# Attention on one core: the product of probabilities and ones set directly behind the product with the values

## The chip, the cores and the metric

One core of a Trainium2 chip runs the kernel. The metric is device time in microseconds (us), the median of several runs. Five engines work side by side and meet through semaphores: TensorE (PE, with its weight loads shown as PEld), VectorE (DVE), ScalarE (ACT), GpSimd (POOL) and the DMA queues, most of them fed by SyncE (SP).

## The reference

The layer is a gated cross-attention followed by a gated mixture of experts, over 8 sequences of 512 tokens of width 512. The change touches the attention alone:

```python
Q = proj(query, Wq, bq); K = proj(key, Wk, bk); V = proj(value, Wv, bv)   # 16 heads of 32
scores = jnp.einsum('bhqd,bhkd->bhqk', Q, K) / SCALE
attn = jax.nn.softmax(scores, axis=-1)
out = jnp.einsum('bhqk,bhkd->bhqd', attn, V)
...
x = x + jnp.tanh(g_xattn[0]) * _L0_xattn_ref(_layernorm(x), ctx_1024, ctx_1024, ...)
x = x + jnp.tanh(g_ffn[0]) * _L0_ffn_ref(_layernorm(x), ...)   # router, top 2 of 8 experts
```

## The kernel before

The program first runs the attention for 8 batches one after another (batch 0, a loop over batches 1 to 6, batch 7), then the router and the 8 experts. The order of every engine's work is written out by hand.

A batch of the attention begins with the projections of queries and keys. They are split into two float16 parts and stacked by DMA in `stk`, so that one matmul of 96 rows gives the scores of a head in full precision. Then come 23 steps, s = 0 to 22 (`SLOTS`), and after them the output product (L1346). A step holds work of three ages:

- `scores(s, qt)` (L1227), for s below 16: head s, 128 queries x 512 keys. There are four of them, qt = 0 to 3, each of one matmul, and they write only two PSUM banks: qt 0 and 2 bank 0, qt 1 and 3 bank 1. DVE takes the row maxima out of each (`mx`, L838) and frees the bank; before TensorE writes the next scores there, `claim` makes it wait for that.
- `less_maxima(u, hf)` (L1237), u = s - 6: the transposed scores with the maxima already taken off, for a group of four heads and 128 keys, in two halves of two matmuls. ACT turns each half into probabilities `pt` (the exponential, L718). The halves write banks 2 and 3, and 4 and 5.
- `with_values` (L1246) and `with_ones` (L1253), v = s - 7: the probabilities of the step before times the values, into bank 6, and times ones, which gives the sums of the softmax, into bank 7. Each has one matmul for each of the four heads of the group; each of these writes 32 partitions, and the four stand in four column tiles of the array. They are float32, and the trace counts each as two instructions. The last one of `with_ones` raises `pv_done`.

Ahead of `with_values` TensorE waits until ACT has read both halves of the step before (`copied`), and in steps 11, 15 and 19, where a new group of heads begins, until ACT has copied banks 6 and 7 to `osum` (L726). That copy stands on ACT behind both exponentials of its step, 10, 14 and 18 (L718 first, then L726).

In steps 4, 8, 12 and 16 a transpose of the maxima (L1318) goes through bank 0 as well; DVE reads it in two instructions (L859, L861) that stand between its maxima of qt 0, 1 and of qt 3, 2. In these steps TensorE computes qt 3 ahead of qt 2. In steps 16 to 22 of all batches but the last, TensorE also transposes the inputs of the next batch (L1154). DVE further has the reciprocals of the sums (L850), the product with them (L878) and the statistics of the next batch.

Of the kernel before, what the change touches and what calls it, by code (L numbers as in the profile page):

```python
# [43 lines left out]
LAG_B, LAG_C = 6, 7  # L44
# [39 lines left out]
def layer_kernel(nc, x, ctx_in, g_x, g_f, Wq, bq, Wk, bk, Wv, bv, Wo, bo, Wr, br, W1, b1, W2, b2, out):  # L84
# [8 lines left out]
    with stack:  # L93
# [195 lines left out]
        def copied(eng, where, key, b=0):  # L289

            bank, n = where(key, b)
            eng.wait_ge(bank_read[bank], n + 1)
# [850 lines left out]
        def _(pe):  # L1143
# [68 lines left out]
            def batch(b, last_batch, first=False):  # L1212
                rows, parts, logits = router(use, b, KT * b)
                for i, (which, m) in enumerate(QK_ORDER):
                    n = "qk".index(which)
                    if m == 0:
                        for kt in range(KT):
                            copied(pe, act_use, ("actT", n, kt), b)
                    dst, full = claim(pe, use, ("qk", i), b)
                    product(dst, [(wT[:, n, wp, kt, m * P:(m + 1) * P], actT[:, n, xp, kt, :])  # L1220
                                  for kt in range(KT) for wp, xp in PARTS]).then_inc(full, 1)

                def scores(s, qt):

                    if s < UNITS:
                        dst, full = claim(pe, use, ("S", s, qt), b)
                        t_.matmul(dst, stk[0:96, 0, s, qt * P:(qt + 1) * P], stk[0:96, 1, s, :],  # L1227
                                  start=True, stop=True).then_inc(full, 1)

                def less_maxima(u, hf):  # L1230

                    if 0 <= u < UNITS:
                        g, kt = u // 4, u % 4
                        _, full = claim(pe, use, ("ST", u, hf), b)
                        for j in range(2):
                            h = 4 * g + 2 * hf + j
                            last = t_.matmul(psum[:, 2 + 2 * hf + j, :], stk[0:98, 1, h, kt * P:(kt + 1) * P],  # L1237
                                             stk[0:98, 0, h, :], start=True, stop=True)
                        last.then_inc(full, 1)

                def with_values(u):
                    if 0 <= u < UNITS:
                        g, kt = u // 4, u % 4
                        for j in range(4):
                            h = 4 * g + j
                            t_.matmul(psum[32 * j:32 * j + 32, 6, :], v32[:, kt, HD * h:HD * h + HD],  # L1246
                                      pt[:, (2 * u + j // 2) % 4, j % 2, :], start=(kt == 0), stop=(kt == KT - 1))

                def with_ones(u):
                    if 0 <= u < UNITS:  # L1250
                        kt = u % 4
                        for j in range(4):
                            last = t_.matmul(psum[32 * j:32 * j + 32, 7, :], ones32[:, :],  # L1253
                                             pt[:, (2 * u + j // 2) % 4, j % 2, :], start=(kt == 0), stop=(kt == KT - 1))
                        last.then_inc(pv_done, 1)

                def values(tt, half):

                    if half == 0:
                        claim(pe, use, ("v", tt), b)  # L1260
                    bank, _ = use(("v", tt), b)
                    for kt in (2 * half, 2 * half + 1):
                        for xp, wp in PARTS:
                            last = t_.matmul(psum[:, bank, :], actT[:, 1, xp, kt, tt * P:(tt + 1) * P], wT[:, 2, wp, kt, :],
                                             start=(kt == 0 and (xp, wp) == (0, 0)),
                                             stop=(kt == KT - 1 and (xp, wp) == (1, 0)))
                    if half == 1:
                        last.then_inc(bank_full[bank], 1)

                if first:  # L1270
                    pe.wait_ge(k_ones, 1)
                for s in range(SLOTS):

                    if s == 0:
                        pe.wait_ge(stk_q0, 12 * 16 * b + 12 * 16)
                    if s < 4:
                        pe.wait_ge(stk_k0[s], 3 * 16 * b + 3 * 16)
                    if s == 4:
                        dmas = (12 + 3 * len(SP_HEADS)) * 16
                        pe.wait_ge(stk_rest, dmas * b + dmas)  # L1280
                        dmas = 3 * len(POOL_HEADS) * 16
                        pe.wait_ge(stk_rest_pool, dmas * b + dmas)
                    scores(s, 0)
                    scores(s, 1)
                    if s == X2T_SLOT:
                        rows()
                    for tt in range(KT):
                        if s in V_HALF[tt]:
                            values(tt, V_HALF[tt].index(s))
                    if s == LG_SLOT:  # L1290
                        parts()
                    u = s - LAG_B
                    if 0 <= u < UNITS and u % 4 == 0:
                        pe.wait_ge(mrow_in[u // 4], 32 * b + 32)
                    less_maxima(u, 0)
                    if not last_batch and s > UNITS:
                        for i in act_tiles(s):
                            inputs_transposed(b + 1, i // KT, i % KT)
                    if 0 <= s - LAG_C < UNITS:
                        v_ = s - LAG_C  # L1300
                        if v_ < KT:
                            copied(pe, use, ("v", v_), b)
                        if v_ % 4 == 0:

                            if v_ == 0:
                                pe.wait_ge(norm_done, NG * b)
                            else:
                                pe.wait_ge(osum_ready, (NG - 1) * b + v_ // 4)
                        for hf in range(2):
                            copied(pe, use, ("ST", v_, hf), b)  # L1310
                    with_values(s - LAG_C)
                    if s % 4 == 0 and 4 <= s <= UNITS:
                        g = s // 4 - 1

                        for qt in (2, 3):
                            copied(pe, use, ("S", 4 * g + 3, qt), b)
                        dst, full = claim(pe, use, ("mT", g), b)
                        t_.transpose(dst[0:16, 0:P], mx[:, 16 * g:16 * g + 16], ident[:, :]).then_inc(full, 1)  # L1318
                    if not last_batch and s == UNITS:
                        for i in act_tiles(s):  # L1320
                            inputs_transposed(b + 1, i // KT, i % KT)
                    if s % 4 == 0:

                        less_maxima(u, 1)
                        scores(s, 3)
                        scores(s, 2)
                    else:
                        scores(s, 2)
                        less_maxima(u, 1)
                        scores(s, 3)  # L1330
                    for tt in range(KT):
                        if V_HALF[tt] == (s, s):
                            values(tt, 1)
                    if s == LG_SLOT:
                        logits()
                    with_ones(s - LAG_C)
                for gs in (range(KT - 1), range(KT - 1, KT)):
                    for tt in range(KT):
                        if gs[0] == 0:
                            claim(pe, use, ("o", tt), b)  # L1340
                        bank, _ = use(("o", tt), b)
                        for kt in gs:
                            if tt == 0:
                                pe.wait_ge(a_ready, NG * b + kt + 1)
                            for ap, wp in PARTS:
                                last = t_.matmul(psum[:, bank, :], aT[:, ap, kt, tt * P:(tt + 1) * P], wT[:, 3, wp, kt, :],  # L1346
                                                 start=(kt == 0 and (ap, wp) == (0, 0)),
                                                 stop=(kt == KT - 1 and (ap, wp) == (1, 0)))
                        if gs[0] == KT - 1:
                            last.then_inc(bank_full[bank], 1)  # L1350
# [146 lines left out]
```

## Time and profile before

| | us |
|---|---|
| median of 3 runs | 2117.45 |
| range of the 3 runs | 2116.48 to 2123.11 |
| span of the profiled execution, first to last instruction | 2114.6 |
| median less that span | 2.85 |
| PE busy | 1856.6 (88%) |
| DVE busy | 1260.1 (60%) |
| ACT busy | 690.7 (33%) |
| POOL busy | 743.9 (35%) |

The page gives no time of the profiled execution beyond its span. The attention fills about the first 990 us; the router and the experts follow. A busy share is a mean over the whole span, so what matters for one step of the attention has to be read from the order in time inside that step.

### The profile page before, as it was taken

The page shows a single profiled execution, that of the slowest core. Times are in us where ns is not written, and L with a number is a line of the kernel's source. Part 1 is how long each engine was busy: PE and PEld are TensorE (multiplying, and loading weights), DVE is VectorE, ACT ScalarE, POOL GpSimd, SP SyncE. Part 2 cuts the span into 40 slices and gives each one's busy share as a digit, 9 for nine tenths or more (in the row PEclk, how much of TensorE's full clock was granted, in tenths as well). Part 3 has the DMA queues.
Part 4 walks back from the last instruction along what each step waited for, and adds up shares of the span by engine and source line. Part 5 has one row for each costly group of instructions (what it writes and reads, how often), then busy time and mean ns, then how long its engine had stood idle before and what let it go on. Part 6 is the DMA issues. An engine that isn't in the chain of part 4 may idle for free. (4 is left out here: it accounts for less than half of the span.)

```text
span 2114.6 us, 31511 instructions
## 1 busy us (share of the span) xinstructions
PE 1856.6 (88%) x10838; PEld 956.6 (45%) x10838; DVE 1260.1 (60%) x2128; ACT 690.7 (33%) x884; POOL 743.9 (35%) x650
## 2 busy tenths in 40 slices
PE   7999999999999999996029898998988988898996
PEld 4333242423333242422016565565655656565674
DVE  5776768686776868675856445462544635445330
ACT  4443535344443536343204123031321303123030
POOL 2424233433424233412324334242442524334241
PEclk9999999999999999998559999999999999999998
DMA  5214131211314131222201324223342322324211
GB/s 184 61 43 118 41 102 38 78 62 52 107 40 119 40 84 36 49 72 78 88 24 61 95 79 129 64 78 81 92 110 63 118 57 92 96 78 128 64 41 25
DMA packets 116959, 162.23 MB, mean 77 GB/s; under 512 B 45236, under 2 KB 63040, under 8 KB 112808
## 3 DMA queue, kind: packets, MB, share of 16 engines
q1 hardware_dynamic: 72488, 134.00, 20.0%
q0 software_dynamic: 44416, 27.50, 6.8%
q8 instruction: 34, 0.56, 0.1%
q14 instruction: 21, 0.17, 0.0%
HBM read 108.92 MB, written 26.85 MB: 64 GB/s over the span
## 5 line engine op out<-in xcount | busy, mean ns | idle before, releaser
L1429 PE MATMUL psum<-xgT,w 128*128 128x308 f16 (+1 forms) x3072 | 437.8, 300 | 3.8 <-ACT h L768 3.2
L1451 PE MATMUL psum<-w,hT 128*123 128x512 f16 x1920 | 433.0, 387 | 3.3 <-PE psum L1391 3.3
L838 DVE TENSOR_REDUCE mx<-psum 128x1 f32<-128x512 f32 x512 | 328.8, 684 | 151.5 <-PE psum L1227 150.3
L1429 PEld LDWEIGHTS psum<-xgT,w 128*128 128x128 f16 x3072 | 296.5, 99 | 116.4 <-ACT h L768 3.5
L1451 PEld LDWEIGHTS psum<-w,hT 128*123 128x123 f16 x1920 | 263.2, 139 | 159.2 <-issue 15.2
L628 POOL TENSOR_TENSOR hT<-h,hT 128x615 f16<-128x615 f32 x128 | 221.2, 1728 | 278.0 <-DVE hT L1106 278.0
L718 ACT ACTIVATE pt<-psum 128x1024 f32<-128x1024 f32 x256 | 259.3, 1022 | 171.1 <-PE psum L1237 171.1
L768 ACT ACTIVATE h<-psum,b1c 128x308 f32<-128x308 f32 (+1 forms) x256 | 117.7, 514 | 539.5 <-PE psum L1429 485.6
L638 POOL DMA_INDIRECT out_dram<-y,idx_now x40 | 102.3, 2558 | 331.5 <-DVE y L1134 243.2
L1227 PE MATMUL psum<-stk 96*128 96x512 f16 x512 | 173.0, 384 | 33.3 <-DVE mx L838 14.3
L1106 DVE CAST hT<-h 128x615 f16<-128x615 f32 x128 | 63.3, 495 | 198.5 <-ACT h L768 198.5
L752 ACT ACTIVATE w<-stage 128x2048 f16<-128x2048 f32 x64 | 122.2, 1909 | 177.0 <-DMA stage<-in_L_ffn_W_dram 177.0
L1149 PE MATMUL psum<-actT,wT 128*128 128x512 f16 x768 | 167.1, 379 | 2.0 <-DVE wT L825 2.0
L1081 DVE SCALAR_TENSOR_TENSOR w<-stage,w 128x512 f16<-128x512 f32 x240 | 165.8, 722 | 0.3
L1061 DVE TENSOR_SCALAR hot<-iota_p,p_e 128x123 bf16<-128x123 bf16 x256 | 162.2, 722 | 0.0
L1237 PE MATMUL psum<-stk 98*128 98x512 f16 x512 | 153.6, 381 | 0.0
L1131 DVE SCALAR_TENSOR_TENSOR y<-psum,b2b 123x512 f32<-123x512 f32 x40 | 27.7, 692 | 198.0 <-PE psum L1451 198.0
L1246 PE MATMUL psum<-pt,v 128*32 128x512 f32 x1024 | 136.4, 605 | 5.3 <-ACT osum L726 5.0
L1253 PE MATMUL psum<-pt,ones 128*32 128x512 f32 x1024 | 136.2, 604 | 0.0
L541 POOL TENSOR_SCALAR a<-t,bias 128x512 f32<-128x512 f32 x32 | 22.3, 697 | 317.2 <-DVE t L878 317.2
L1227 PEld LDWEIGHTS psum<-stk 96*128 96x128 f16 x512 | 43.9, 96 | 198.2 <-DVE mx L838 132.4
L1086 DVE COPY xgT<-psum 128x615 f16<-128x615 f16 x64 | 28.9, 479 | 149.5 <-PE psum L1406 149.1
(177 smaller groups left out, 1860.6 us busy)
## 6 DMA issues: line engine op xcount, KB each, us to landing
stage<-in_L_ffn_W_dram SPq DMA_DIRECT2D x64, 1024.0 KB, 5.3
stk<-qks SPq DMA_DIRECT2D x120, 96.0 KB, 2.8
xin<-in_x_dram SPq DMA_DIRECT2D x8, 1024.0 KB, 5.1
cin<-in_ctx_dram SPq DMA_DIRECT2D x8, 1024.0 KB, 5.3
xres<-in_x_dram SPq DMA_DIRECT2D x8, 1024.0 KB, 5.7
out_dram<-xres SPq DMA_DIRECT2D x32, 256.0 KB, 2.1
x_split<-x2hl SPq DMA_DIRECT2D x32, 256.0 KB, 2.2
stk<-qks POOLq DMA_DIRECT2D x72, 96.0 KB, 3.8
```

The costliest lines, as they stand in the source:

```text
L628: g.tensor_tensor(hT[:, 1, m, :], h32[:, m % 4, :], hT[:, 0, m, :], ALU.subtract).then_inc(h_ready, 1)
L718: s.activation(pt[:, (2 * u + hf) % 4, :, :], psum[:, bank:bank + 2, :], ACT.Exp, scale=1.0 / (math.sqrt(HD) * SQ * SQ)).then_inc(read, 1)
L838: v.reduce_max(mx[:, KT * t + qt:KT * t + qt + 1], ps, AX.X).then_inc(read, 1)
L1061: v.tensor_scalar(hot[:, t % HOT, :], iota_p[:, :], p_e[:, t:t + 1], None, ALU.is_equal).then_inc(hot_ready, 1)
L1081: v.scalar_tensor_tensor(part[1], stage[:, i % 2, cols], SW, part[0], ALU.mult, ALU.subtract).then_inc(chunk_split, 1)
L1149: last = t_.matmul(dst, lhsT, rhs, start=(i == 0), stop=(i == len(pairs) - 1))
L1227: t_.matmul(dst, stk[0:96, 0, s, qt * P:(qt + 1) * P], stk[0:96, 1, s, :], start=True, stop=True).then_inc(full, 1)
L1237: last = t_.matmul(psum[:, 2 + 2 * hf + j, :], stk[0:98, 1, h, kt * P:(kt + 1) * P], stk[0:98, 0, h, :], start=True, stop=True)
L1246: t_.matmul(psum[32 * j:32 * j + 32, 6, :], v32[:, kt, HD * h:HD * h + HD], pt[:, (2 * u + j // 2) % 4, j % 2, :], start=(kt == 0), stop=( ...
L1253: last = t_.matmul(psum[32 * j:32 * j + 32, 7, :], ones32[:, :], pt[:, (2 * u + j // 2) % 4, j % 2, :], start=(kt == 0), stop=(kt == KT - 1))
L1429: mm = t_.matmul(psum[:, (2 * m + ch) % 4, 0:c1 - c0], w1[:, wp, kt, m * P:(m + 1) * P], xgT[:, xp, kt, c0:c1], start=(kt == 0 and (wp, xp ...
L1451: mm = t_.matmul(psum[0:CP, Y_BANK[c], :], hT[:, hp, k, c * CP:(c + 1) * CP], w2[:, wp, k, :], start=(k == 0 and (hp, wp) == (0, 0)), stop ...
```

## The change

`with_ones` of a step is called directly behind `with_values` of the same step and no longer at the end of the step. Nothing is added or removed, and the waits and semaphores of each instruction stay the same.

```diff
@@ -1309,6 +1309,7 @@
                         for hf in range(2):
                             copied(pe, use, ("ST", v_, hf), b)
                     with_values(s - LAG_C)
+                    with_ones(s - LAG_C)
                     if s % 4 == 0 and 4 <= s <= UNITS:
                         g = s // 4 - 1
 
@@ -1333,7 +1334,6 @@
                             values(tt, 1)
                     if s == LG_SLOT:
                         logits()
-                    with_ones(s - LAG_C)
                 for gs in (range(KT - 1), range(KT - 1, KT)):
                     for tt in range(KT):
                         if gs[0] == 0:
```

Only TensorE's queue has another order. On it, a step with scores and the beginning of the next (steps 11 and 12 of a batch) read before, with L1227 the scores, L1237 those with the maxima off, L1246 the product with the values, L1253 that with ones, L1318 the transpose of the maxima:

```order
L1237 MATMUL psum<-stk 128x512 x2
L1246 MATMUL psum<-pt,v 32x512 x4
L1227 MATMUL psum<-stk 128x512
L1237 MATMUL psum<-stk 128x512 x2
L1227 MATMUL psum<-stk 128x512
L1253 MATMUL psum<-pt,ones 32x512 x4
L1227 MATMUL psum<-stk 128x512 x2
L1237 MATMUL psum<-stk 128x512 x2
L1246 MATMUL psum<-pt,v 32x512 x4
L1318 MATMUL psum<-ident,mx 16x128
```

The same place on TensorE after the change (the transpose is now at L1319):

```order
L1237 MATMUL psum<-stk 128x512 x2
L1246 MATMUL psum<-pt,v 32x512 x4
L1253 MATMUL psum<-pt,ones 32x512 x4
L1227 MATMUL psum<-stk 128x512
L1237 MATMUL psum<-stk 128x512 x2
L1227 MATMUL psum<-stk 128x512 x3
L1237 MATMUL psum<-stk 128x512 x2
L1246 MATMUL psum<-pt,v 32x512 x4
L1253 MATMUL psum<-pt,ones 32x512 x4
L1319 MATMUL psum<-ident,mx 16x128
```

The last two scores of a step and the first two of the next, which had the product with ones between them, now stand side by side: the row "x3" holds the fourth score of one step and the first two of the next.

On TensorE in the steps without scores (17 and 18 of a batch that is not the last; L1154 is the transpose of the next batch's inputs), before:

```order
L1237 MATMUL psum<-stk 128x512 x2
L1154 MATMUL psum<-ident,xn 128x128 x4
L1246 MATMUL psum<-pt,v 32x512 x4
L1237 MATMUL psum<-stk 128x512 x2
L1253 MATMUL psum<-pt,ones 32x512 x4
L1237 MATMUL psum<-stk 128x512 x2
L1154 MATMUL psum<-ident,xn 128x128 x4
L1246 MATMUL psum<-pt,v 32x512 x4
```

And after:

```order
L1154 MATMUL psum<-ident,xn 128x128 x4
L1246 MATMUL psum<-pt,v 32x512 x4
L1253 MATMUL psum<-pt,ones 32x512 x4
L1237 MATMUL psum<-stk 128x512 x4
L1154 MATMUL psum<-ident,xn 128x128 x4
L1246 MATMUL psum<-pt,v 32x512 x4
```

Between the second half of the scores with the maxima off and the product with values that needs its exponential, the product with ones no longer stands; what is left there is the next step's first half (in the same row, "x4") and the transpose.

## Rows read from the trace of the kernel before

**Rows 1.** The page: TensorE's busy share and granted clock in 40 slices.

```profile
PE   7999999999999999996029898998988988898996
PEclk9999999999999999998559999999999999999998
```

**Rows 2.** Stretches of the span: engines' busy time, granted clock, DMA share.

```profile
core 0: us, PE busy (x) PEld busy (x) DVE busy (x) ACT busy (x) POOL busy (x), PEclk, DMA share, GB/s
438.87:471.88 33.01, 32.39 (x198) 7.72 (x194) 27.64 (x48) 18.76 (x19) 15.76 (x16) 1.00 0.02 8
471.88:496.14 24.26, 24.09 (x174) 7.57 (x170) 18.71 (x28) 14.26 (x15) 3.72 (x4) 1.00 0.13 44
950.68:972.05 21.37, 20.49 (x141) 3.83 (x138) 8.47 (x12) 14.17 (x15) 3.71 (x4) 1.00 0.01 1
```

**Rows 3.** Timeline, TensorE, one regular step: start, length, what, idle before it.

```profile
443.14 0.60 PE L1227 MATMUL psum<-stk 96*128 96x512 f16 x2
443.59 0.60 PE L1237 MATMUL psum<-stk 98*128 98x512 f16 x2
444.11 1.07 PE L1246 MATMUL psum<-pt,v 128*32 128x512 f32 x8
445.11 0.39 PE L1227 MATMUL psum<-stk 96*128 96x512 f16 x1
445.34 0.60 PE L1237 MATMUL psum<-stk 98*128 98x512 f16 x2
445.77 0.38 PE L1227 MATMUL psum<-stk 96*128 96x512 f16 x1
446.08 1.06 PE L1253 MATMUL psum<-pt,ones 128*32 128x512 f32 x8
447.08 0.39 PE L1227 MATMUL psum<-stk 96*128 96x512 f16 x1
```

**Rows 4.** Timeline, TensorE, end of a batch: the two products side by side.

```profile
494.28 1.06 PE L1246 MATMUL psum<-pt,v 128*32 128x512 f32 x8
495.16 1.04 PE L1253 MATMUL psum<-pt,ones 128*32 128x512 f32 x8
496.14 1.04 PE L1346 MATMUL psum<-wT,aT 128*128 128x512 f16 x4
```

**Rows 5.** Timeline, TensorE, end of step 5 and start of step 6.

```profile
430.91 0.60 PE L1227 MATMUL psum<-stk 96*128 96x512 f16 x2
432.07 0.39 PE L1227 MATMUL psum<-stk 96*128 96x512 f16 x1 [0.57 <-DVE mx L838]
432.67 0.39 PE L1227 MATMUL psum<-stk 96*128 96x512 f16 x1 [0.21 <-DVE mx L838]
```

**Rows 6.** Timeline: first users of a score and of a second half, and reciprocals.

```profile
445.54 0.69 DVE L838 TENSOR_REDUCE mx<-psum 128x1 f32<-128x512 f32 x1 [0.30 <-PE psum L1227]
446.03 1.02 ACT L718 ACTIVATE pt<-psum 128x1024 f32<-128x1024 f32 x1 [0.79 <-PE psum L1237]
454.99 0.94 DVE L850 RECIPROCAL osum<-osum 128x128 f32<-128x128 f32 x1
```

**Rows 7.** Timeline, step 8: the transpose of the maxima and what follows it.

```profile
440.83 0.28 PE L1318 MATMUL psum<-ident,mx 128*16 128x128 f32 x1
441.79 0.10 PEld L1227 LDWEIGHTS psum<-stk 96*128 96x128 f16 x1 [0.53 <-DVE mrow L861]
441.80 0.69 DVE L838 TENSOR_REDUCE mx<-psum 128x1 f32<-128x512 f32 x1
```

**Rows 8.** Timeline, step 11: ACT's copy of the sums and TensorE's wait.

```profile
451.23 1.02 ACT L726 ACTIVATE osum<-psum 128x1024 f32<-128x1024 f32 x1 [0.24 <-PE psum L1253]
452.15 1.02 ACT L718 ACTIVATE pt<-psum 128x1024 f32<-128x1024 f32 x1
452.31 0.64 PE L1246 MATMUL psum<-pt,v 128*32 128x512 f32 x4 [0.25 <-ACT osum L726]
```

**Rows 9.** Timeline, TensorE, last batch: a second half, and the values that need it.

```profile
968.33 0.60 PE L1237 MATMUL psum<-stk 98*128 98x512 f16 x2
968.86 1.06 PE L1253 MATMUL psum<-pt,ones 128*32 128x512 f32 x8
970.20 1.06 PE L1246 MATMUL psum<-pt,v 128*32 128x512 f32 x8 [0.27 <-ACT pt L718]
```

**Rows 10.** The page: the count of the moved instructions.

```profile
L1253 PE MATMUL psum<-pt,ones 128*32 128x512 f32 x1024 | 136.2, 604 | 0.0
```

## The prediction

> **What bounds the kernel now.** I read the slices first: during the attention TensorE is busy 90% or more in nearly every slice, at a granted clock of 1.00, so at the 2.4 GHz level [rows 1, 2]. The chain that ended last covers only 4% of the span and says nothing of the attention. So I went to the stretches and the timeline. Steps 8 to 15 of a batch take 33.01 us, with TensorE busy 32.39; steps 16 to 22 take 24.26 us with 24.09 busy [rows 2]. TensorE is the bound there, and nobody delivers late. The reader should then see why nobody is late. In a regular step (3.94 us from 443.14 to 447.08) two tiled products of 1.0 us each stand between pairs of scores [rows 3]. The scores have two banks only. While the product with values runs, DVE empties the banks of qt 0 and 1; while the product with ones runs, it empties those of qt 2 and 3. The same product also covers ACT's exponential of the second half. The change takes this second cover away and puts it on top of the first.
>
> **What the change gives.** The 1,024 counted instructions [rows 10] are 8 per step, 128 steps, 16 per batch. Alone, a tiled product takes 1.00 us until the next float16 matmul starts (444.11 to 445.11) and 0.09 more ahead of it (the pair from 443.59 takes 0.52 where the one from 445.34 takes 0.43) [rows 3]. Side by side the first takes 0.88 and the second 0.98, together 1.86 [rows 4]; I use 1.87. So TensorE's own work falls by 2.00 + 0.09 - 1.87, about 0.22 us a step. Step 22 has the two side by side already, so 15 steps of a batch move: 15 x 8 x 0.22 = 26 us to be won if nothing waits.
>
> The Trainium skill (TensorEngine Tiling (Array Packing), Key Properties) says that changing the tiling mode drains the engine. The 0.12 and 0.09 us above bear it out, and by that rule alone the change should be faster; that is my first rival.
>
> **What it costs in steps with scores (7 to 15).** Between steps 5 and 6 no product stands yet: the last two scores of step 5 start at 430.91, the first of step 6 follows 1.16 us later (432.07) and its second 0.60 after that (432.67), each waiting for DVE [rows 5]. That is the neighbourhood that the change makes in the later steps, with the same banks in the same turn (the fourth score there comes 0.66 behind the third, still in time for DVE's second reading). So I take 1.16 from the third score of a step to the first of the next and 1.76 to its second. Before, the distances were 1.97 (445.11 to 447.08) and about 2.2, and no wait showed. The relative times of a regular step are now: first score 0, second 0.60 (held by DVE; 0.22 if free), first half 0.82, values 1.34 (0.52 later), both products 1.87, third score 3.21, next first score 3.21 + 1.16 = 4.37. Against 3.94 that is +0.43.
>
> - A step with the transpose (8, 12): it starts at 3.21, and DVE can begin on the scores behind it 0.97 later, at 4.18 (441.80 - 440.83, [rows 7]). The second half fills 3.32 to 3.75 and the fourth score starts at 3.76. In this turn the next first score needs the bank that is read second: 3.76 + 1.76 = 5.52. Its own second score is then free as well, so the step after (9, 13) has it at 0.22: values 0.96, third score 2.83, next step at 3.99.
> - Steps 11 and 15 wait for the copy of sums. It stands on ACT behind the exponential of the second half. That exponential starts 0.69 behind its matmuls (446.03 - 445.34) [rows 3, 6]; the next on ACT follows 0.92 later (452.15 - 451.23), and values may start 1.08 behind the copy's start (452.31 - 451.23) [rows 8]. So values start no sooner than 0.69 + 0.92 + 1.08 = 2.69 after the second half, 2.92 after the third score (0.23 between them). Unheld they would start 1.16 + 1.34 = 2.50 after it. +0.43, so the step takes 4.80. The earlier end of the product with ones doesn't help, since the copy is queued behind the later exponential.
> - Steps 8 to 15: 5.52 + 3.99 + 4.37 + 4.80 + 5.52 + 3.99 + 4.37 + 4.52 (step 15 ends without a next score: 3.64 + 0.88) = 37.08, against 33.01: +4.07. Step 7: third score 0.87 later, next step 1.16 behind it instead of 1.97: +0.06. Together +4.13 per batch.
>
> **What it costs in steps 16 to 22.** There, values wait for the exponential of the last second half: 1.87 us from the start of its matmuls to values (968.33 to 970.20), the wait showing as ACT pt [rows 9]. TensorE has 0.44 (rest of the half) + 0.44 + 0.53 (next half, transposes of the inputs) = 1.41 to fill it, so it idles 0.46. From one second half to the next: 1.87 + 1.87 = 3.74 (about 3.5 before); in step 19, with the copy of sums, 2.69 + 1.87 = 4.56. From the start of step 16: its values at +1.22 (1.87 behind a half that started 0.65 earlier), its second half at 1.22 + 1.87 + 0.11 + 0.44 = 3.64, then 3.74 + 3.74 + 4.56 + 3.74 + 3.74 to that of step 21 at 23.16, values of step 22 at 25.03, output product at 26.89. Against 24.26: +2.63. In the last batch there are no transposes: 1.22 + 1.87 + 0.11 = 3.20, + 19.52 = 22.72, + 1.87 + 1.86 = 26.45, against 21.37: +5.08 [rows 2].
>
> **The sum.** 7 x (4.13 + 2.63) + (4.13 + 5.08) = 47.3 + 9.2 = 56.5 us. The span would go from 2114.6 to 2171.1; the median of the runs lies 2.85 above the profiled span, so 2174. Of this the won 0.22 us a step is already taken off. DVE's and ACT's queues and all DMAs keep their order, and steps 0 to 6, the projections and everything behind the attention are untouched. The output product needs the same last sums in the same order. The transpose of the maxima and the mrow DMA behind it move later in their step, but the steps that use them, two on, move too.
>
> **Bounds.** The weakest terms are those where DVE or ACT has other work. Behind the maxima of step 11 come two reciprocals; one takes 0.94 [rows 6]. The maxima end 1.76 behind the third score, so the reciprocals end near 3.6, the next two maxima near 4.9, and the transposed maxima of step 12 are ready at 1.16 + 3.21 + 0.28 = 4.65: up to 0.25 late, or nothing. I take nothing; 0.25 to 0.5 in four steps of each batch is up to 16 us. To the other side, the distances of ACT could be shorter by 0.1 in the ten held steps, and the waits for the copy may be met halfway: up to 8 x 2 = 16 us.
>
> **Rivals.**
> 1. *Faster, through the spared switches.* For it: the 0.22 us a step, read from rows. It decides if DVE frees a bank within the 0.88 us that TensorE then needs from a third score to the next first one (0.23 + 0.43 + 0.22), instead of 1.16, and the second within 1.10 instead of 1.76. Against it stand both distances behind step 5 [rows 5]. It would give 2117.45 - 26 = 2091.
> 2. *Only the banks count, the ACT side is absorbed.* The +4.13 of steps 7 to 15 stays less the 0.43 in two steps, and steps 16 to 22 go on as before because the transposes and the next half cover the exponential: 8 x 3.3 = 26, so 2144. Against it: 1.41 of cover to 1.87 needed.
> 3. *DVE falls behind for good.* The reciprocals and the statistics now collide with earlier scores, and the upper bound holds or is passed: 2190 and above. For it: DVE is busy 27.64 of 33.01 us [rows 2]; against it: the new step is longer, 37.08, for the same work.
> 4. *The clock.* More gaps in TensorE's work could cost the granted clock. The rows show 1.00 throughout, TensorE's short waits of step 5 among them; it falls only where TensorE's busy digit falls to 6 and 0, behind the attention [rows 1]. If it fell, it would be tens of us more.
> 5. *No change*: waits and spared switches cancel. They would have to be equal, and the rows give 0.43 against 0.22 at least, after the gain is counted.
>
> **Chances.** Forecast (2160 to 2188): 0.74. Rival 1: 0.05. Rival 2: 0.09. Rivals 3 and 4: 0.10. Rival 5: 0.02. The range 2152 to 2191 leaves the lower part of rival 2, rival 1 and most of 4 outside. Within 0.3% (6.4 us) is about what a measurement can tell from no change. Faster 0.05, same 0.02, slower 0.93.
>
> **What would show it.** The third score to the next first one at 1.16 us, with a wait for DVE's maxima of 0.3 us, and 0.4 us ahead of the second; a regular step of 4.37, one with a transpose of 5.52; values held by ACT pt for 0.4 us in steps 17, 18, 20 and 21 and by the copy of sums for some 1.3 us in step 19; values to ones 0.88. In the grouped lines, idle time of TensorE ahead of L1227 should rise from DVE by roughly 8 x 5 us, and PE's busy time should fall by some 25. If regular steps take 3.7 us the prediction is wrong and rival 1 right; if steps 16 to 22 still take 24 us, rival 2.

## The result, and the profile after

The changed kernel takes 2181.57 us (median of 4 runs, 2177.17 to 2185.44), the kernel before 2116.97 beside it: a ratio of 1.0297, 95% interval 1.0273 to 1.0321. That is 64.6 us more, where 57 had been forecast (2174, range 2152 to 2191). In a later series the same pair gave 2180.41 to 2120.4, a ratio of 1.0276 (1.0259 to 1.0294), 60.0 us more. The profiled execution has a span of 2183.5 us, 68.9 above the one of before. It is the slowest of its four (2185.44, 3.9 above the median), so about 4 of the 68.9 us are the choice of the execution.

The page's slices after, TensorE's busy share and granted clock, to be held against [rows 1]: the busy share is 8 in many slices of the attention that had 9, and the attention is longer.

```profile
PE   7898898989889898988306999898988988898997
PEclk9999999999999999999656999999999999999999
```

The same three stretches as in [rows 2], in the profile after (steps 8 to 15, steps 16 to 22, steps 16 to 22 of the last batch):

```profile
462.92:500.22 37.30, 32.51 (x194) 9.05 (x195) 27.43 (x47) 18.38 (x19) 15.70 (x16) 1.00 0.02 5
500.22:527.02 26.80, 23.00 (x171) 9.13 (x169) 20.03 (x30) 14.90 (x16) 3.72 (x4) 1.00 0.13 39
1010.25:1036.60 26.35, 19.48 (x139) 5.25 (x137) 9.56 (x14) 14.79 (x16) 3.71 (x4) 1.00 0.00 1
```

The first is 37.30 us long against 33.01 and the second 26.80 against 24.26. TensorE was idle in them for 0.62 and 0.17 us before and is idle for 4.8 and 3.8 now, while its busy time in the second falls by 1.1 and in the first rises by 0.1. In the last batch the stretch is 26.35 us long against 21.37.

The grouped lines of TensorE before, of the scores and the product with values:

```profile
L1227 PE MATMUL psum<-stk 96*128 96x512 f16 x512 | 173.0, 384 | 33.3 <-DVE mx L838 14.3 <-DMA stk<-qks 12.0 <-DVE mrow L861 4.3
L1246 PE MATMUL psum<-pt,v 128*32 128x512 f32 x1024 | 136.4, 605 | 5.3 <-ACT osum L726 5.0 <-ACT pt L718 0.3
```

And after; the line numbers of these three didn't change:

```profile
L1227 PE MATMUL psum<-stk 96*128 96x512 f16 x512 | 181.9, 386 | 68.0 <-DVE mx L838 42.1 <-DMA stk<-qks 13.0 <-DVE mrow L861 4.3
L1246 PE MATMUL psum<-pt,v 128*32 128x512 f32 x1024 | 136.4, 603 | 37.6 <-ACT pt L718 23.3 <-ACT osum L726 14.4
L1253 PE MATMUL psum<-pt,ones 128*32 128x512 f32 x1024 | 134.5, 592 | 0.0
```

The moved instructions [rows 10] still wait for nobody. The waits are in front of their neighbours: the scores wait 42.1 us for DVE's maxima instead of 14.3, and the product with values waits 37.6 us for ACT instead of 5.3, 23.3 of it for the exponentials and 14.4 for the copy of the sums. The wait for DMA, 13.0, is nearly what it was (12.0).

Steps 9 to 11 on TensorE after, which answer to [rows 3] (start, length, what, and the idle time just before):

```profile
469.50 1.06 PE L1246 MATMUL psum<-pt,v 128*32 128x512 f32 x8
470.38 1.04 PE L1253 MATMUL psum<-pt,ones 128*32 128x512 f32 x8
471.36 0.39 PE L1227 MATMUL psum<-stk 96*128 96x512 f16 x1
471.58 0.60 PE L1237 MATMUL psum<-stk 98*128 98x512 f16 x2
472.02 0.91 PE L1227 MATMUL psum<-stk 96*128 96x512 f16 x2
473.19 0.39 PE L1227 MATMUL psum<-stk 96*128 96x512 f16 x1 [0.26 <-DVE mx L838]
473.41 0.60 PE L1237 MATMUL psum<-stk 98*128 98x512 f16 x2
473.94 1.07 PE L1246 MATMUL psum<-pt,v 128*32 128x512 f32 x8
...
478.71 1.07 PE L1246 MATMUL psum<-pt,v 128*32 128x512 f32 x8 [0.26 <-ACT osum L726]
```

Values to ones is 0.88 us as in [rows 4]. The third score starts at 471.36. The row "472.02 ... x2" holds two scores that do not follow one another at once: its length of 0.91 instead of 0.60 is the wait for the first bank (0.14), folded in, and the second of the two starts at 472.53. The next step's second score starts at 473.19, 1.83 behind the third score. A step from values to values is 4.44 us (469.50 to 473.94) and, with the wait for the copy, 4.77 (473.94 to 478.71). It was 3.94 and 4.26.

Step 8 after, which answers to [rows 7]:

```profile
466.22 0.28 PE L1319 MATMUL psum<-ident,mx 128*16 128x128 f32 x1
...
466.77 0.80 PE L1227 MATMUL psum<-stk 96*128 96x512 f16 x2
468.53 0.60 PE L1227 MATMUL psum<-stk 96*128 96x512 f16 x2 [0.96 <-DVE mx L838]
```

From the score of qt 3 (466.77), which this step computes ahead of qt 2, to the next first one (468.53) there are 1.76 us, with 0.96 of plain waiting. Steps 17 to 19 after, the answer to [rows 9] for a batch with transposes:

```profile
505.70 1.07 PE L1246 MATMUL psum<-pt,v 128*32 128x512 f32 x8 [0.40 <-ACT pt L718]
506.56 1.07 PE L1253 MATMUL psum<-pt,ones 128*32 128x512 f32 x8
507.56 1.04 PE L1237 MATMUL psum<-stk 98*128 98x512 f16 x4
508.43 0.60 PE L1154 MATMUL psum<-ident,xn 128*128 128x128 f32 x4
509.43 1.06 PE L1246 MATMUL psum<-pt,v 128*32 128x512 f32 x8 [0.39 <-ACT pt L718]
...
513.98 1.06 PE L1246 MATMUL psum<-pt,v 128*32 128x512 f32 x8 [1.22 <-ACT osum L726]
```

Each step takes 3.73 us instead of 3.50, and values wait 0.4 us for the exponential; in step 19 they wait 1.22 us for the copy.

Because the four transposes of the maxima (steps 4, 8, 12, 16) and the output product show in every batch, their starts cut each batch into stretches that can be compared between runs. A length says what the change costs only over a whole batch: where the product with ones of step 8 or 16 is moved, it stands ahead of that step's transpose, so 0.9 us is counted one stretch earlier, and where the values are late, they stand behind it and count one stretch later. Lengths in us, of batches 1 to 6, where they agree within 0.03, and of batch 7; the last column is how many batches from 1 on show a granted clock of 0.5 for 3.4 us behind the DMA wait of step 4:

| kernel | 4 to 8 | 8 to 12 | 12 to 16 | 16 to output | sum | batch 7, sum | at 0.5 |
|---|---|---|---|---|---|---|---|
| before | 13.92 | 16.51 | 16.07 | 22.72 | 69.22 | 66.17 | 0 |
| changed | 15.28 | 18.78 | 18.29 | 23.73 | 76.08 | 75.61 | 3 |
| only steps 7 to 15 | 15.28 | 18.78 | 17.43 | 22.72 | 74.21 | 71.22 | 0 |
| only steps 16 to 22 | 13.92 | 16.52 | 16.92 | 23.73 | 71.09 | 72.13 | 0 |
| changed, half first | 14.46 | 17.51 | 17.48 | 23.73 | 73.18 | 72.76 | 1 |
| changed, short maxima | 13.64 | 17.41 | 17.31 | 23.73 | 72.09 | 71.62 | 1 |
| before, short maxima | 12.68 | 16.38 | 15.87 | 22.72 | 67.65 | 64.65 | 5 |
| changed, copy first | 15.28 | 18.45 | 17.95 | 23.24 | 74.92 | 74.38 | 1 |
| both at the end | 13.78 | 16.50 | 15.73 | 22.20 | 68.21 | 63.70 | 0 |
| values late, with step 7 | 14.57 | 16.15 | 14.71 | 22.21 | 67.64 | 63.12 | 1 |
| values late, without step 7 | 13.92 | 16.15 | 14.71 | 22.20 | 66.98 | 63.35 | 1 |

For the changed kernel this gives 6 x 6.86 + 9.44 (batch 7) + 6.94 (batch 0, 75.98 to 69.04) = 57.5 us. Of the other 11.4 us between the two spans, 1.35 lie ahead of batch 0's step 4, 5.7 between an output product and step 4 of the next batch (seven times) and 4.4 behind the attention. The 1.35 go with the clock as well: the changed kernel's profile has 3.4 us at 0.5 there, behind a wait of 1.99 us for DVE. Nine of the thirteen profiles have them, with step 4 of batch 0 at 68.27 to 70.33 us; the other four, the one of before among them, have the same wait without them, and step 4 at 67.02 to 67.98.

### The profile page after: what moved, and what is told of

Same layout as the page of the kernel before. It is cut to its first block and busy times, and to the rows that moved or that the text cites. A ratio compares the mean times of both kernels' runs of the same rounds, so it can differ in the third digit from the quotient of the medians.

```text
span 2183.5 us, 31511 instructions
## 1 busy us (share of the span) xinstructions
PE 1858.8 (85%) x10838; PEld 982.2 (45%) x10838; DVE 1259.4 (58%) x2128; ACT 685.5 (31%) x884; POOL 743.8 (34%) x650
## 5 line engine op out<-in xcount | busy, mean ns | idle before, releaser
L1227 PE MATMUL psum<-stk 96*128 96x512 f16 x512 | 181.9, 386 | 68.0 <-DVE mx L838 42.1
L1246 PE MATMUL psum<-pt,v 128*32 128x512 f32 x1024 | 136.4, 603 | 37.6 <-ACT pt L718 23.3
L1227 PEld LDWEIGHTS psum<-stk 96*128 96x128 f16 x512 | 48.0, 96 | 219.5 <-DVE mx L838 123.8
L1237 PE MATMUL psum<-stk 98*128 98x512 f16 x512 | 146.6, 380 | 0.0
L1253 PE MATMUL psum<-pt,ones 128*32 128x512 f32 x1024 | 134.5, 592 | 0.0
L1149 PEld LDWEIGHTS psum<-actT,wT 128*128 128x128 f16 x768 | 75.3, 98 | 94.0 <-issue 4.4
```

The lines of the kernel that those rows point to most:

```text
L1149: last = t_.matmul(dst, lhsT, rhs, start=(i == 0), stop=(i == len(pairs) - 1))
```

## The experiments

**The change in half of the steps.** With the scores (steps 7 to 15) and without them (16 to 22), as two kernels; the diff is the first, and the second has the two conditions exchanged.

```diff
                     with_values(s - LAG_C)
-                    with_ones(s - LAG_C)
+                    if s < UNITS:
+                        with_ones(s - LAG_C)
...
+                    if s >= UNITS:
+                        with_ones(s - LAG_C)
```

> The product with ones stands directly behind the product with values only in steps below 16, where scores are left; in steps 16 to 22 it stands as in the kernel before. Bank theory (the scores have two banks, and DVE's maxima no longer finish behind a product): regular steps of 4.44 us instead of 3.94, those with the transpose of the maxima near 5.7, +4.3 us a batch, so +34 us in all, near 2151, with TensorE's waits in steps 16 to 22 gone. Rival (the two tiled products side by side are themselves slow): the loss goes by the number of moved steps, 9 of 15, so +39 us. Rival (only the exponential counts): near 0.

Measured: 2161.29 us to 2119.2, ratio 1.020 (1.0178 to 1.0221), +42.1 (40.0 in the stretches). The mechanism's +34 was too low, and the rival that the pair is slow (+39) isn't refuted by this run alone; the last batch of the next run and the kernel with both products at the end decide against it.

> The reverse: moved only in steps 16 and up. Exponential theory: values wait 0.4 us in steps 17, 18, 20, 21 and 22 and 1.2 us in step 19; +2.5 us in each of seven batches and +5 in the last, which has no transposes to fill the gap: +23 us, near 2140. Rival (the pair itself is slow, per step): 6 of 15 steps, +26 us, but the last batch like the others. Rival (only the banks count): -10 us, the spared changes of tiling.

Measured: 2139.78 us to 2119.2, ratio 1.0091 (1.007 to 1.0113), +20.6. In its last batch, where no transposes fill the gap, the trace shows

```profile
984.29 1.04 PE L1237 MATMUL psum<-stk 98*128 98x512 f16 x4
986.17 1.06 PE L1246 MATMUL psum<-pt,v 128*32 128x512 f32 x8 [0.83 <-ACT pt L718]
```

a wait of 0.83 us where the other batches have 0.4. The two parts add up (4.99 + 1.87 = 6.86 a batch; 42.1 + 20.6 = 62.7 us in all), so they don't act on each other. The tail's loss follows the gap, 1.87 us in six batches and 5.96 in the last, and not the number of moved steps: the same six steps move in each. Of the 5.96, some 1.65 is half clock in that batch (24.94 us from step 16 to the output, 23.29 in the changed kernel at full clock), so the gap costs 4.3. The split is 5.0 to 1.9 a batch where 4.3 to 2.5 was expected. I had booked the wait at step 16 under the tail, but it comes whenever step 15 has its product with ones moved: with steps 7 to 15 alone, the values of step 16 wait 0.61 us for the exponential.

**Other work into the gap.** The changed kernel, with the first half ahead of the first two scores.

```diff
+                    u = s - LAG_B
+                    if 0 <= u < UNITS and u % 4 == 0:
+                        pe.wait_ge(mrow_in[u // 4], 32 * b + 32)
+                    less_maxima(u, 0)
                     scores(s, 0)
                     scores(s, 1)
...
-                    less_maxima(u, 0)
```

> The changed kernel, with the first half of the scores with the maxima off put ahead of the first two scores of each step, so that 0.44 us of other work stands where TensorE waits for DVE. Bank theory: the step of 4.44 us falls to 4.00, in steps that do not wait for the copy of sums; about 6 steps of a batch x 0.44 x 8 = 21 us back, near 2160, and steps 16 to 22 as in the changed kernel. Rival (the pair of products is slow in itself, or the waits only look like DVE's): no change from 2182.

Measured: 2150.61 us, ratio to before 1.0142 (1.0118 to 1.0166); the changed kernel had 1.0297 and 1.0276. A regular step on TensorE:

```profile
458.95 0.39 PE L1227 MATMUL psum<-stk 96*128 96x512 f16 x1
...
459.83 0.59 PE L1237 MATMUL psum<-stk 98*128 98x512 f16 x2
460.27 0.90 PE L1227 MATMUL psum<-stk 96*128 96x512 f16 x2
461.10 1.07 PE L1246 MATMUL psum<-pt,v 128*32 128x512 f32 x8
461.98 1.04 PE L1253 MATMUL psum<-pt,ones 128*32 128x512 f32 x8
462.95 0.39 PE L1227 MATMUL psum<-stk 96*128 96x512 f16 x1
```

It takes 4.00 us (458.95 to 462.95), as the bank account says: the same DVE wait, partly filled. The stretches give 2.9 us a batch, 23 in all, against 21 expected; the medians differ by some 30, of which the rest lies outside the stretches, some 4 of it the half clock behind step 4's wait (one batch against three). Steps 16 to 22 are unchanged (23.73).

**A faster DVE.** Both orders with maxima over 128 of the 512 keys; the maxima of the other keys are left out.

```diff
-                            v.reduce_max(mx[:, KT * t + qt:KT * t + qt + 1], ps, AX.X).then_inc(read, 1)
+                            v.reduce_max(mx[:, KT * t + qt:KT * t + qt + 1], ps[:, 0:128], AX.X).then_inc(read, 1)
```

> The changed kernel, but DVE takes the maxima over the first 128 of 512 keys only (the maxima of the other keys are left out), so that it frees a bank some 0.4 us sooner. Bank theory: the third score to the next first one takes 0.88 instead of 1.16 us (TensorE's own work), the next second one waits 0.25 instead of 0.43, a regular step 3.95 instead of 4.44, the one with the transpose 4.9 instead of 5.74; the steps with scores cost 1 us a batch more than before instead of 4.3, steps 16 to 22 still +2.5. Against the kernel before with the same short maxima: +28 us instead of +65. Rival (the product pair, or TensorE's queue, is what is slow): still +60 or more.

> The kernel before with the same short maxima over 128 keys (the maxima of the other keys are left out), as the base for the run with the changed order. Both theories: regular steps stay at 3.94 us, since the product with ones covers DVE anyway; only the steps with the transpose of the maxima and steps 1 to 7 gain, together up to 2 us a batch: 2100 to 2115.

Measured: 2149.57 us (1.0132, 1.0114 to 1.0151) and 2116.83 (0.9976, 0.9964 to 0.9987) to 2121.44, the second above the 2100 to 2115 expected. The order alone now costs 32.7 us, about half, where 28 had been expected. From the first of the two:

```profile
454.24 0.39 PE L1227 MATMUL psum<-stk 96*128 96x512 f16 x1
...
455.67 0.39 PE L1227 MATMUL psum<-stk 96*128 96x512 f16 x1 [0.17 <-DVE mx L838]
...
456.42 1.07 PE L1246 MATMUL psum<-pt,v 128*32 128x512 f32 x8
...
461.19 1.07 PE L1246 MATMUL psum<-pt,v 128*32 128x512 f32 x8 [0.66 <-ACT osum L726]
```

From the third score to the next second one there are 1.43 us instead of 1.83, and the regular step is 4.04 us (452.38 to 456.42, the values of steps 9 and 10) instead of 4.44; 3.95 had been expected. Where values wait for the copy nothing is gained: the step stays at 4.77 and the wait grows from 0.26 to 0.66, since ACT's copy ends 2.9 us behind the third score whatever DVE does. Against the kernel before with short maxima, the stretches 4 to 16 cost 3.4 us more. Of that 0.9 is the place of step 16's product with ones, ahead of the transpose, which leaves 2.5 for the steps with scores, not the 1 us that I had expected: the two waits for the copy, in steps 11 and 15, cost 0.5 and 0.6 more than there (steps of 4.77 to 4.26 and 4.18), and values of step 16 wait 0.61 for the exponential. The other 0.8 is not accounted for. By the stretches the order still costs 7 x 4.4 + 7.0 = 38 us, where it cost 57.5; the medians differ by less, and in the profile of the kernel before with short maxima the DMA wait of step 4 is 2.3 to 2.9 us long and the clock falls behind it in five batches, about 1.7 us each, against one in the other.

**The copy of the sums earlier on ACT.** The changed kernel with `osum` between the two exponentials of its step.

```diff
+                        if t in GROUP_END[:-1] and hf == 0:
...
+                            s.activation(osum[:, :, :], psum[:, 6:8, :], ACT.Copy).then_inc(osum_ready, 1)
-                    if t in GROUP_END[:-1]:
...
-                        s.activation(osum[:, :, :], psum[:, 6:8, :], ACT.Copy).then_inc(osum_ready, 1)
```

> The changed kernel, with ACT's copy of the sums ahead of the second exponential of its step instead of behind it. Queue theory (in steps 11, 15 and 19 values wait for the copy only because it stands behind a late exponential): no wait in steps 11 and 15 (0.26 us each), in step 19 values start 2.2 instead of 2.7 us behind the second half: 1 us a batch, 8 in all, near 2173. Rival (the copy is late because ACT is short of time): no change.

Measured: 2167.87 us, ratio to before 1.0224 (1.0203 to 1.0245). In step 10 ACT now does

```profile
471.05 1.02 ACT L725 ACTIVATE osum<-psum 128x1024 f32<-128x1024 f32 x1 [0.94 <-PE psum L1252]
471.97 1.02 ACT L718 ACTIVATE pt<-psum 128x1024 f32<-128x1024 f32 x1
```

and values of step 11 start without a wait. The stretches shrink by 0.33, 0.34 and 0.49 us, 1.16 a batch, 9 us in all (8 expected); the medians differ by 12.5 (to 2180.41, the changed kernel beside another set of runs). In step 19 values still wait 0.73 us, now for the exponential. ACT had time; its order was the cause of the waits for the copy.

**The pair side by side with its cover kept.** The kernel before, with both products at the end of every step; the waits of the product with values move with it.

```diff
...
-                    with_values(s - LAG_C)
...
                     if s == LG_SLOT:
                         logits()
+                    with_values(s - LAG_C)
                     with_ones(s - LAG_C)
```

> The two products side by side as in the changed kernel, but both at the end of the step: the one with values moves, not the one with ones. In a regular step the first half fills part of DVE's wait, so 4.00 us; steps with the transpose of the maxima 4.6; no wait for the copy of sums; in steps 16 to 22 the exponentials have a whole step, so 3.28 instead of 3.50 us. Cover theory (bank and exponential): -1.5 us a batch in steps 16 to 22, about 0 in the others, near 2105. Rival (two tiled products side by side are slow): near 2180.

Measured: 2110.71 us to 2119.2, ratio 0.9957 (0.9941 to 0.9972). A regular step:

```profile
444.77 0.61 PE L1227 MATMUL psum<-stk 96*128 96x512 f16 x2
445.22 0.60 PE L1237 MATMUL psum<-stk 98*128 98x512 f16 x2
445.95 0.39 PE L1227 MATMUL psum<-stk 96*128 96x512 f16 x1
...
446.92 1.06 PE L1246 MATMUL psum<-pt,v 128*32 128x512 f32 x8
447.81 1.04 PE L1253 MATMUL psum<-pt,ones 128*32 128x512 f32 x8
448.78 0.39 PE L1227 MATMUL psum<-stk 96*128 96x512 f16 x1
```

With this the rival that the pair itself is slow falls. The pair takes 1.86 us here as well (446.92 to 448.78) and the step 4.01: the 0.22 us saved go to a wait of the third score for DVE, which starts 1.18 us behind the first (444.77 to 445.95) though only 0.88 us of work stand between, but little more is lost. The gain comes from steps 16 to 22 and from the vanished wait for the copy. Near 2105 had been expected, with 1.5 us a batch won in steps 16 to 22; they won 0.5, and 1.2 in the last batch.

**The better version.** From that: the values late only where a wait or a free ACT makes it pay, first in steps 7, 11, 15 and 16 to 22, then without step 7. The diff is the second; the first has `s % 4 == 3` in place of `s in (11, 15)`. The waits of the product with values move with it, as above.

```diff
+                    late = s >= UNITS or s in (11, 15)
+                    if not late:
+                        with_values(s - LAG_C)
...
+                    if late:
+                        with_values(s - LAG_C)
                     with_ones(s - LAG_C)
```

> The kernel before, with the product with values moved down to the one with ones (both at the end of the step) only in steps 7, 11, 15 and 16 to 22; elsewhere the order of before. Cover theory: the pair saves its 0.22 us only where something else covers DVE and ACT. Steps 11 and 15 lose the wait for the copy of sums (4.00 instead of 4.26), steps 16 to 22 gain 0.5 us as with both products at the end everywhere, regular steps stay at 3.94: 1.3 us a batch, 11 us in all, near 2107. Rival (with both products at the end everywhere, the gain came from regular steps): smaller than that run's gain of 8.5 us.

Measured: 2109.43 us to 2121.44, ratio 0.9943 (0.9927 to 0.9959). Its 4-to-8 stretch is 0.65 us longer than before, and its trace tells why:

```profile
433.68 0.39 PE L1227 MATMUL psum<-stk 96*128 96x512 f16 x1 [0.26 <-DVE mx L838]
433.90 0.60 PE L1237 MATMUL psum<-stk 98*128 98x512 f16 x2
435.22 0.39 PE L1227 MATMUL psum<-stk 96*128 96x512 f16 x1 [0.72 <-DVE mx L838]
```

Step 7 is the first with products and comes straight from the uncovered step 6, so DVE is still behind; it needs the values in the middle.

> The kernel before, with the product with values moved down to the one with ones in steps 11, 15 and 16 to 22 (and not in step 7, where the run with step 7 too showed steps 7 and 8 0.3 us longer in spite of what step 11 saves). Cover theory: 0.6 us a batch less than with step 7 moved too, near 2105. Rival (step 7 is indifferent, the difference is where the transpose of the maxima stands): 2109 as that run.

Measured: 2099.1 us (2096.35 to 2104.64) to 2120.4, ratio 0.9892 (0.9873 to 0.991): 21 us faster than the kernel before and 81 than the changed one. The stretches account for 6 x 2.24 + 2.82 + 2.15 (batch 0) = 18.4 of the 21. Near 2105 had been expected. The direction of the step 7 theory holds, but its size is open: the stretches of the two kernels differ by some 4 us, their medians by 10.

**The clock behind the DMA wait.** In the changed kernel's profile, batch 4, step 4, and TensorE's mean clock in the stretch behind it (in a row of stretches the last three figures are granted clock, DMA share and GB/s):

```profile
574.91 0.60 PE L1227 MATMUL psum<-stk 96*128 96x512 f16 x2 [1.91 <-DMA stk<-qks]
575.35 2.65 PE L1264 MATMUL psum<-wT,actT 128*128 128x512 f16 x6
577.92 1.51 PE L1199 MATMUL psum<-x2nT,wr 128*32 128x512 f32 x8
```

```profile
575.00:579.00 4.00, 4.00 (x16) 1.10 (x15) 1.29 (x2) 0.00 (x0) 0.00 (x0) 0.57 0.00 0
```

Six matmuls take 2.65 us instead of 1.46. The same happened in batches 1 and 7.

> The changed kernel again, on this chip. Phase theory of the clock (three batches of its first profile ran at a granted clock of 0.5 for 3.4 us behind the wait for DMA in step 4, 1.9 us each, which batches does not depend on the order): other batches or another number of them show it, and the steps 4 to 22 of every batch are the same to 0.1 us; median 2180 to 2186. Rival (the change causes these three): the same batches 1, 4 and 7 again.

Measured: 2180.41 us, ratio 1.0276. All stretches from step 4 on are the same to 0.11 us, the sums to 0.02 but for batches 5 and 7 (76.18 to 76.07 and 75.53 to 75.60); the low clock came in batches 1 and 5. So it is not bound to a batch. The last kernel is the changed one with eight more matmuls, whose result nobody uses, ahead of that wait:

```diff
                     if s == 4:
+                        for _ in range(8):
+                            t_.matmul(psum[:, 5, :], actT[:, 1, 0, 0, 0:P], wT[:, 2, 0, 0, :], start=True, stop=True)
                         dmas = (12 + 3 * len(SP_HEADS)) * 16
```

> The changed kernel with 8 matmuls of 128x512 float16 (1.75 us, their result is not used) put ahead of the wait for the stacked heads in step 4, where TensorE stands idle for 1.6 to 2.3 us. Idle theory of the clock: no stretch of granted clock 0.5 in any batch from 1 on, and the wait is only filled, so 0 to 5 us less than the changed kernel, 2176 to 2182. Rival (the clock falls for another reason): the stretches stay. If the wait is shorter than the filling, up to 0.2 us a batch more.

Measured: 2181.94 us (2178.06 to 2182.68), ratio 1.0283 (1.0265 to 1.03). With the wait filled,

```profile
571.82 1.89 PE L1280 MATMUL psum<-wT,actT 128*128 128x512 f16 x8
...
574.17 1.46 PE L1264 MATMUL psum<-wT,actT 128*128 128x512 f16 x6
```

the clock stays at 1.00 in all batches from 1 on, and an output product is 50.4 to 50.6 us ahead of the next step 4. This agrees with the idle time as the cause of the low clock but doesn't show it: it is one profile, and four of the twelve profiles without the filling have no such stretch either. The end of the attention came at 1032.0 us instead of 1034.0, but the median didn't move: two or three such stretches in a run are within its spread.

## Why the prediction was right

*The spared changes of tiling.* 0.22 us a step, there in every trace: values to ones 0.88, ones to scores 0.98 (0.86 and 1.00 in most of steps 16 to 22). The Trainium skill (TensorEngine Tiling (Array Packing), Key Properties) says that a change of tiling mode drains the engine. The trace shows no drain as such, but a price at the changes that agrees: some 0.12 us between and 0.09 ahead. The 0.09 isn't one of the number type: before, four float32 transposes of the whole array take 0.44 us ahead of a float16 half (473.53 to 473.97) and 0.53 ahead of the tiled values (475.93 to 476.46). For the 0.12 no run separates the two. The price is a third of the waiting that took its place: a regular step became 0.50 us longer in spite of the 0.22 saved, so 0.72 us of waits came in.

*The bank distances.* 1.16 and 1.76 were taken from [rows 5]; measured are 1.17 (471.36 to 472.53, where the weights of the next first score are loaded) and 1.83. The second was 0.07 short, because the fourth score comes 0.66 behind the third here and DVE waits for it a moment. Regular step 4.37 forecast, 4.44 measured; behind the transpose 3.99 to 4.00; the transpose's own step 5.52 to 5.61 (the score that the prediction calls the fourth there is qt 3, the third computed, and its 1.76 is right for that one); with the copy 4.80 to 4.77. Steps 8 to 15: 37.08 to 37.30. The filled gap moves the regular step to the 4.00 us that this account gives and the short maxima to 4.04 (3.95 forecast), which shows the cause.

*The exponential's cover.* Steps 16 to 22: 26.89 forecast, 26.80 measured. In the last batch, without transposes, 26.45 forecast and 26.35 measured.

*The copy of the sums.* Right in size (2.69 behind the second half, 2.69 measured at 476.02 to 478.71) and in cause: it goes when ACT's order is changed.

*The signs.* Two came out differently. The idle time ahead of L1227 put down to DVE rose by 28 us and not by some 40; another 6 of its rise stand with no releaser named, like the 0.14 at 472.53. And PE's busy time did not fall by 25: it rose from 1856.6 to 1858.8. At half clock L1264 and L1199 are 5.2 us longer, and in steps 8 to 15 no fall shows though a product pair is 0.22 shorter. There a score ahead of a wait counts with its whole 0.39 us, where 0.22 later the next one starts when nothing waits. That reading is not tested, but it says where to look for such a saving: in the distances between rows and not in the busy sum.

*The sum.* 56.5 forecast, 57.5 measured in the stretches that the change touches. The term of 2.85 on top mixed a median with the span of another execution; within one execution it is 1.9. The medians rose by 64.6 and by 60.0 in the two series, so 2.5 to 7 us came from outside the sum, which has no term for them. Rival 1 falls by both distances; rival 2 by the +1.9 us a batch that moving steps 16 to 22 alone costs; rival 3 did not come: TensorE's regular steps stay equal through the reciprocals. Rival 5 is out of question. Of rival 4 a small part was true, in a place where I hadn't looked: not in the new gaps of 0.3 to 1.2 us but behind the old wait for DMA in step 4, which already stood at 1.61 to 1.87 us in the kernel before. Some 6 us of the profile's difference are that, and the 1.35 at the start; since the number of such batches changes from run to run (3 and 2 here, 0 in the one profile of before), how much of it the change causes stays open. So does the 4.4 us behind the attention. What lies there takes 1142.5 us before and 1146.9 after, but between 1138.5 (the changed order with short maxima) and 1149.8 in the thirteen profiles, so a difference of 4.4 between two single profiles can't be laid on the change.

## What to carry to other kernels

Work that seems free to move is often someone's cover. Before two like operations are put together, work out, for each pair of neighbours that comes together instead, how long the buffer between them takes to come free; where the reader is slower than the writer, as DVE was here with two banks, independent work must stand on both sides. If the saving at the seam is still wanted, group the operations where a wait would have stood anyway, and leave the others apart: here that gave 21 us less than before in place of 64.6 more.

## What the runs showed of the hardware

- Eight float32 instructions in four column tiles, followed by eight more in the same tiling, take 0.88 us and the last eight 0.98 (0.86 and 1.00 in most of steps 16 to 22); between full-array matmuls each eight cost 1.00 + 0.09.
- From a float16 score of 512 columns, read by a DVE maximum over 128x512, to the next score in the same bank there are 1.17 us; the second bank, read behind it, gets its next score 1.76 (step 8) to 1.83 us after that start. With maxima over 128x128 the second distance is 1.43.
- ACT starts successive operations of 128x1024 every 0.92 us, though each is shown as 1.02 us long.
- A granted clock of 0.5 for 3.4 us followed waits for DMA of 1.88 to 2.9 us in some batches and not in others as long (with: 2.10 us, half first; without: 2.09, only steps 7 to 15, and 2.81, before with short maxima). In the run with only steps 16 to 22 moved it also came inside the last batch, behind a wait of 1.66 us for the copy together with others of 0.83; the same waits in the last batch of the changed kernel were followed by none. The length of a wait alone doesn't decide it.
